# Output scatters of a routed expert layer that wait for one another's landing, in place of a lag counted in tiles

## The reference

```python
t = x.reshape(-1, d)                                  # 1024 tokens of 128
logits = t @ switch_w + switch_b
route_prob = jax.nn.softmax(logits, axis=-1)
routes = jnp.argmax(route_prob, axis=-1)
for e in range(8):
    y = jax.nn.gelu(t @ w1[e] + b1[e]) @ w2[e] + b2[e]    # 128 -> 512 -> 128
    out = jnp.where((routes == e)[:, None], y, out)
out = out * route_prob_max[:, None]
x = x + out                                           # the result
```

## Time and profile before

| what | us |
|---|---|
| median of 3 executions | 201.17 |
| lowest and highest of them | 200.12, 201.94 |
| span of the profiled execution, first to last instruction | 199.1 |

### The profile page before, as it was taken

The page is one execution under the profiler, slowest core; times in us unless marked ns, Lnnn a source line. Parts: engine busy times, 40 slices in busy tenths (PEclk is TensorE's granted clock), DMA queues, the critical chain, the costliest instruction groups (busy, mean ns, idle before and its releaser), DMA issues.

```text
span 199.1 us, 3287 instructions
## 1 busy us (share of the span) xinstructions
PE 167.0 (84%) x881; PEld 115.6 (58%) x881; DVE 120.9 (61%) x360; ACT 97.5 (49%) x228; POOL 63.7 (32%) x74
## 2 busy tenths in 40 slices
PE   7885899989988888689989999956789799998930
PEld 2533655565647345465754554622689799998830
DVE  2799837769741959775274995546585465454420
ACT  5490448655631653423168346460453776637520
POOL 8899060002100092020001002064008446455541
PEclk9999589999999997999999999999969999999995
DMA  6400007000001999900000000012702450000100
GB/s 190 151 3 4 4 6 244 2 1 5 5 3 20 290 392 507 340 2 0 3 0 0 0 0 0 3 55 91 253 7 84 143 188 25 25 10 4 34 12 2
DMA packets 14482, 15.47 MB, mean 78 GB/s; under 512 B 6842, under 2 KB 11205, under 8 KB 14400
## 3 DMA queue, kind: packets, MB, share of 16 engines
q1 hardware_dynamic: 12944, 13.29, 20.7%
q0 software_dynamic: 1088, 1.60, 2.5%
q10 hardware_dynamic: 432, 0.37, 0.8%
HBM read 13.50 MB, written 5.44 MB: 95 GB/s over the span
## 4 chain that ended last, share of the span: by engine, by line
PE 58%; DVE 21%; issue 7%; ACT 6%; DMA 3%; POOL 2%; ACTq 1%; SPq 0%; DVEq 0%; POOLq 0%; another core or an unknown queue 0%
PE scores L1074 13%; PE acc L981 9%; PE acc L1085 8%; PE scores L966 4%; PE shared L1028 4%; DVE MR L732 4%; DVE QG L722 3%; PE shared L941 3%; PE shared L1014 3%; PE acc L879 3%; PE shared L921 2%; PE shared L893 2%; PE shared L988 2%; PE shared L1001 2%; DVE XN L684 2%
## 5 line engine op out<-in xcount | busy, mean ns | idle before, releaser
L981 PE MATMUL acc<-P,VP 123*128 123x512 f32 (+1 forms) x80 | 41.1, 612 | 0.6 <-ACT P L596 0.6
L596 ACT ACTIVATE P<-scores 123x512 f32<-123x512 f32 (+1 forms) x40 | 23.0, 595 | 22.5 <-PE scores L966 22.1
L642 ACT ACTIVATE HT<-scores,B 128x128 f32<-128x128 f32 x88 | 25.3, 372 | 14.0 <-PE scores L1074 10.9
L732 DVE TENSOR_REDUCE MR<-shared 128x4 f32<-128x308 f32 x64 | 26.8, 471 | 4.3 <-PE shared L941 4.0
L518 POOL DMA_INDIRECT out<-XS,token x22 | 21.4, 973 | 19.2 <-DVE XS L860 14.2
L1074 PE MATMUL scores<-XST,HT 128*128 128x128 f32 x176 | 24.8, 285 | 2.7 <-ACT XST L635 2.6
L941 PE MATMUL shared<-KG,QG 98*128 98x308 f32 x64 | 22.1, 409 | 3.4 <-DVE QG L722 1.3
L504 POOL TENSOR_TENSOR X<-X,ROWS 128x512 f32<-128x512 f32 x6 | 8.1, 1345 | 52.5 <-DVE XN L684 52.3
L1085 PE MATMUL acc<-W,HT 128*128 x176 | 23.8, 281 | 1.2 <-ACT HT L642 1.2
L1074 PEld LDWEIGHTS scores<-XST,HT 128*128 128x128 f32 x176 | 22.2, 198 | 4.1 <-ACT XST L635 3.7
L966 PE MATMUL scores<-QG,KG 102*123 102x512 f32 (+1 forms) x48 | 23.2, 531 | 1.3 <-ACT QG L588 0.5
(11 more groups left out here) (120 smaller groups left out, 234.0 us busy)
## 6 DMA issues: line engine op xcount, KB each, us to landing
W<-in_w SPq DMA_DIRECT2D x16, 256.0 KB, 6.9
slots<-in_empty SPq DMA_DIRECT2D x1, 2860.0 KB, 14.5
XS<-slots SPq DMA_DIRECT2D x2, 650.0 KB, 6.1
XS<-slots SPq DMA_DIRECT2D x2, 390.0 KB, 3.8
W<-in_ffn0w SPq DMA_DIRECT2D x1, 534.0 KB, 5.6
XS<-slots SPq DMA_DIRECT2D x2, 260.0 KB, 3.0
X<-in_x SPq DMA_DIRECT2D x2, 256.0 KB, 4.5
B<-in_b SPq DMA_DIRECT2D x1, 512.0 KB, 4.7
```

What stands on the lines that cost most here:

```text
L596: act.activation(P[0:w, n % NP], scores[n % 2][0:w, :], ACT.Exp).then_inc(probs_ready, 1)
L642: ins = act.activation(HG1[:, t % NHB, c], hidden[t % 2][:, c], ACT.Gelu_apprx_tanh, bias=B1[:, bass.ds(expert[t] * NF + k, 1)])
L732: dve.tensor_reduce(MR[:, b, qt, g, 2:2 + HG], bank(s)[:, 0:GK].rearrange("p (h k) -> p h k", h=HG), AX.X, ALU.max).then_inc(max_read, 1)
L981: pe.matmul(acc[half][:, :], VP[0:w, l, b, j, half], P[0:w, n % NP, :], start=(j == 0), stop=(j == NT - 1)).then_inc(probs_used, 1)
```

## The change

The list of lags is gone. Each output scatter waits for its own tile's result alone. The scatters of the tiles 1 to 18 wait in addition until `stored` has reached 16 t, which is when all t scatters ahead of them have landed. Scatter 0 and the last three (19, 20 and 21) have no such wait.

```diff
-LAG = [2] * 7 + [1] * 7 + [0] * (NS - 14)
+LAST = 3
...
                     t = s[1] - 2
-                    pool.wait_ge(z_ready, t + 1 + LAG[t])
+                    pool.wait_ge(z_ready, t + 1)
+                    if 0 < t < NS - LAST:
+                        pool.wait_ge(stored, 16 * t)
                     pool.indirect_dma_start(out, bass.IndirectOffsetOnAxis(ap=token[:, t:t + 1], axis=0), XS[:, t, 0:D], None,
                                             bounds_check=B * S - 1, oob_is_err=False).then_inc(stored, 16)
```

## The result

The changed kernel takes 225.1 us (median of 4 executions, 224.83 to 227.81), the kernel before 201.56 (4 executions beside them). The ratio is 1.121, with a 95% interval of 1.114 to 1.128: slower. The forecast was 220.9 us, and the range of 215.5 to 226.0 holds the time. The profiled execution has a span of 223.0 us against 199.1.

What follows compares the result with a forecast made beforehand. The expert loop of PE and DVE was taken to set the end. Scatter 2 at 163.5, sixteen periods of 2.9, 3.8 for the last three and 5.03 of tail gave span 218.8, time 220.9 us; range 215.5 to 226.0.

Steps and rivals of the forecast that it cites:

- The chain and what it bounds: Output scatters on POOL: each of 1 to 18 waits for the previous landing, period 2.9 us against DVE's 2.0.
- The landing: From an output scatter's start on POOL to its landing: 2.1 us, the middle of 1.8 and 2.35.
- the hand-over: From a scatter's landing to the next one's start on POOL: 0.8 us, with 0.30 as lower bound.
- Scatter 1 in the load traffic: Scatter 1, started at 157.8, waits behind SP's second-batch loads and lands at 162.7; 2.8 us less if it doesn't.
- 1 us for tiles that take longer: Allowance in the range's upper end, 226.0, for tiles slowed by the last of the load traffic.
- The end: Scatters 19 to 21 take three steps of 1.28 us, 3.8 in all, then a fixed tail of 5.03 us.
- An early signal: Rival: `stored` reaches 16 t early, period 1.76 us, landing not exposed, 201.2 us; chance 0.04.
- a hand-over of 0.30: Rival of a shorter chain: landing to next start costs 0.30, period 2.4 us, time 212.9 us; chance 0.05.
- a landing of 2.75 for each: Rival of a longer chain: each output scatter lands as slowly as the rank scatter, time 231.3 us; chance 0.06.
- PE's and DVE's last instructions should stay near 192: Expected in the changed profile: the expert loop ends near 192 us, about as before.
- nobody waits for a scatter: Output scatters: source isn't reused and target isn't read, so an earlier scatter frees nothing.

Runs made afterwards that it cites:

- Two in flight: The changed kernel, but each scatter waits for the landing of the one two before, on two semaphores in turn: 202.25 us, ratio 1.0121.
- wait and lags: The kernel before with the landing wait added and its lags kept: 225.72 us, ratio 1.117.
- LAST = 12: The changed kernel with only scatters 1 to 9 waiting for a landing, 10 to 21 not: 210.38 us, ratio 1.040.
- the lag of 3: The kernel before with each scatter waiting for the result three tiles on (capped at the last), no landing wait: 201.08 us, ratio 1.0037.
- all behind the loop: The changed kernel without landing wait, every scatter waiting for the last tile's result: 223.65 us in one execution.
- a lag of 2: The kernel before with each scatter waiting for the result two tiles on (capped at the last), no landing wait: 201.0 us, ratio 0.9975.
- the lag of 3 kept long: The kernel before with lag 3 to tile 13, 2 to 17, 1 for 18 and 19, then 0, no landing wait: 200.55 us, ratio 1.0017.
- two in flight and lags: The changed kernel, each scatter waiting for the landing two before, with lags from 3 to 0 in steps: 201.63 us, ratio 1.0074.
- a lag of 1: The kernel before with each scatter waiting for the next tile's result (capped at the last), no landing wait: 201.6 us, ratio 1.003.
- without lags: The changed kernel without the landing wait, each scatter waiting for its own tile's result alone: 202.94 us, ratio 1.0093.
- lags 3 2 1 0: The kernel before with lag 3 for tiles 0 to 7, 2 to 12, 1 to 17, then 0, no landing wait: 200.74 us, ratio 1.0045.
- groups of four: The kernel before with scatters released in fours behind the group's fourth result (last group two), no landing wait: 208.63 us, ratio 1.0315.

## Why the prediction was right

**The chain and what it bounds.** Right, and shown twice: taking the wait away ends the loss, and shortening the chain by nine scatters takes 14.7 us of it. Two in flight show that it is latency.

**The landing, 2.1 us, and the hand-over, 0.8 us.** Measured 2.12 to 2.15 for tiles that are part full or empty, 2.24 for full ones, and 0.84, so a period of about 2.97 instead of 2.9, and 3.09 for full tiles. Sixteen periods make 1.1 us more than forecast. The choice of 2.1, the middle of two bounds, was in part luck: no row of before showed a landing, and how full a tile is, one of the two reasons given, is worth 0.12 us at most. The Trainium skill's page DMA: Bandwidth & Descriptors, section "Anatomy of one DMA — SWDGE (gpsimd) path", gave an estimate of 2.15 us for 64 KB. The trace has 2.24 us for 64 KB and 2.12 for next to no data, so it agrees within 0.1 us, with a fixed part that is 0.12 us longer than the page's.

**Scatter 1 in the load traffic.** It was costed at 4.9 us to landing; the longest landing measured, which is this one, is 5.6 us. By the trace's list of packets its data moves from 3.8 to 5.2 us behind its start, where the others' begin 1.5 us behind it, so it did wait behind the loads. Rank's last scatter started 1.3 us earlier in this execution (152.03, not 153.33) and scatter 0 at 153.30, not 154.7, so scatter 2 started at 162.71 against a forecast 163.5.

**What was left out.** Three steps are longer than the rest: 3.70 us (168.65 to 172.35), 3.95 (172.35 to 176.30) and 4.68 (182.39 to 187.07), together 3.4 us over three periods of 2.97. That is the larger part of the 4.2 us by which scatter 18 came later than forecast, at 214.10 and not 209.9: 3.4 from these, 1.1 from the period, 0.8 less from the start, and the rest mostly in the steps of full tiles (3.09). The forecast took one landing time for all and had nothing to exclude stragglers but "1 us for tiles that take longer". Windows around the longest, the landing of scatter 8 (last two columns DMA share and GB/s), show a last piece of its data 0.9 us behind the rest:

```profile
183.90:184.30 0.40, 0.40 (x6) 0.40 (x5) 0.24 (x1) 0.00 (x0) 0.00 (x0) 1.00 0.39 117
184.30:185.10 0.80, 0.80 (x10) 0.80 (x9) 0.00 (x0) 0.65 (x3) 0.00 (x0) 1.00 0.00 0
185.10:185.50 0.40, 0.40 (x6) 0.40 (x6) 0.18 (x1) 0.40 (x2) 0.00 (x0) 1.00 0.04 5
```

In the trace's list of packets an instruction packet of 16 KB starts at 183.61 and lasts 1.53 us, and the late piece starts at 185.13, just when it ends. Likewise an instruction packet lies at 173.01 (1.37 us) and one at 170.16 (0.52 us), beside the other two long steps. The packets at 164.62 and 181.80 didn't meet a scatter's data, and the steps there have 2.95 and 3.09 us. The kernels with wait and lags and with LAST = 12 have the same long step between scatters 8 and 9 (182.52 to 187.33, 184.15 to 188.71), with packets at 183.89 and 185.82 in the way of its data. Between scatters 4 and 5, which is a long step here (3.70), the kernel with wait and lags takes 3.06 us, and there the nearest packet (170.65) lay ahead of the data. That a DMA engine was held by the fetch of instructions fits all three traces, but it is argued from the times alone; no run moved the fetches.

That the time stayed in the range is thus partly luck. The upper end, 226.0, was written for a landing of 2.35 us and 1 us for slow tiles, and what used it up were the three long steps, which it didn't foresee. The measured time is 0.9 us below it.

**The end.** Three steps of 1.28 and 5.06 us behind the last scatter's start (forecast 3.8 and 5.03).

**The rivals.** An early signal is refuted by the landings of 2.1 us, a hand-over of 0.30 by 0.84, and a landing of 2.75 for each by the median of 2.2.

**What was wrong.** "PE's and DVE's last instructions should stay near 192" did not hold: they stop at 187. The sentence that nobody waits for a scatter, so that an earlier one frees nothing, was too simple. Nothing waits for a scatter, but scatters in a row hold the loop up. The forecast survived it only because 30 us of scatters lay over it. The lags of the kernel before aren't worthless either: without them, and without the wait, the time is 0.9% longer. That this is the same effect isn't shown.

Two readings were a little off and changed nothing. 39.8 us for 19 tiles are 2.1 us a tile and not 2.0, and a landing of 2.1 puts scatter 0's at 156.8 and not 157.0.

## What to carry to other kernels

A wait for one's own last DMA turns a queue into a chain with the whole latency in each step. Compare landing plus hand-over, not the engine's busy time, with the pace at which the data comes: here 2.97 us against 2.0. With n in flight divide by n; two were enough here to get under the pace (1.5 us a scatter against 1.9). When an estimate multiplies one latency by many steps, allow for some steps in which a part of the data comes late. A chain collects every straggler, while DMAs that overlap can make up for one: with two in flight a step of 2.24 us was followed by one of 1.56. And when a loop gets faster, look at what now comes behind it before counting it as gain: with the lag of 3, a loop shorter by 4.4 us bought 0.5 us in the profiled execution and nothing in the median. Compare the granted clock stretch by stretch too, before a longer loop is put down to one cause: the stall with two in flight brought a stretch at 1.2 GHz behind it.

## What the runs showed of the hardware

**Indirect DMAs in a row hold up TensorE's results.** Loop lengths by how the scatters were released: 37.3 us with all behind the loop, 37.3 with a constant lag of 3 (steps of 1.8 to 1.9 us), 37.4, 38.0 and 38.1 in the three chains with a landing wait (steps of 3 us); 38.8 with a lag of 2 and 39.3 with the lag of 3 kept long; 41.1 with two in flight and lags, 41.6 with a lag of 1, 41.7 before, 42.3 without lags and with lags 3 2 1 0, 43.7 with two in flight; 46.2 in groups of four. Scatters 1.28 us apart in threes or fours beside the loop coincide with gaps of 3 to 5 us between additions, and scatters 1.9 us apart have none. That the spacing is the cause is shown by the groups of four against the lag of 3, where the number of scatters and their work is the same, and so is the time from the last addition to the end, 10.7 us. The loops are 8.9 us apart, of which an estimated 1.7 us is the slower clock behind the first gap. The medians, 208.63 and 201.08 us, agree with it. How it works inside is open. The data moved isn't the measure of it, since 184 KB and 39 KB make gaps of 4.9 and 5.1 us; what POOL does to issue a scatter is left as a candidate. Every kernel also has a gap of 2.8 us or more ahead of the third addition (3.7 without lags, 4.5 with a lag of 1), beside or just behind the four rank scatters; no run spaced those. In the third group of four the addition started at 182.05, during the fourth scatter (181.67 to 182.64), so the hold isn't simply one until the row of scatters has ended.

**The clock fell behind three of the stalls.** PE's granted clock went to 1.2 GHz at 160.1 us with two in flight, at 159.2 with a lag of 1 and at 163.5 in groups of four, for 6.8, 3.4 and 3.4 us. PE had been busy for 2.3 of 5.4, 4.6 of 7.4 and 4.2 of 6.6 us ahead of that. The gaps of the kernel before, of the one without lags and of the one with lags 3 2 1 0 brought no such stretch inside their loops (up to 191.6 us in the last), so the stalls are no effect of the clock.

**A scatter's landing hardly depends on what it carries.** 2.12 us for an empty tile and 2.24 for one of 64 KB.

**Clearing the loop gained no time.** No version was faster than the kernel before beyond its interval; the lag of 2 came nearest at 0.9975 (0.9924 to 1.0025). The executions of one kernel spread over some 2%, and a part of that goes with the mean granted clock: of those of the kernel before beside the lag of 3, one at 199.07 us had 0.971 of full speed and one at 201.72 had 0.954. The traces show the loop of one execution each, so whether the 41.7 us before is typical of it stays open.
